# A first stage on two bank pairs, a Gram matrix on four tiles, and convolutions with their taps in turns

## The reference

```
xn  = layernorm(x)
q,k,v = silu(short_conv4(xn @ W.T))            # 4 heads of 64, causal, 4 taps per channel
beta = sigmoid(xn @ Wb.T)
delta = chunked delta rule on l2norm(q), l2norm(k), v*beta, k*beta   # triangular solves, a scan
local = three causal FIR filters over v, of 3, 15 and 63 taps
p   = softmax((xn @ gate_w + gate_b) / exp(log_temp)), clipped mix with eps
o   = p0*short + p1*mid + p2*long + p3*delta + p4*v ;  o = rmsnorm(o) * norm_w
x1  = x + layernorm(o @ Wo.T)
xr, xk = mixes of layernorm(x1) and its row before
out = x1 + layernorm(sigmoid(xr @ Wr) * (relu(xk @ Wk)^2 @ Wv))
```

## Time and profile before

| | us |
|---|---|
| median of 3 runs | 616.0 (615.16 to 617.41) |
| the profiled execution | 611.72 |
| its span | 609.9 |
| TensorE busy (matmul) | 512.3 |
| TensorE busy (weight load) | 407.8 |
| VectorE busy | 465.3 |
| GpSimd busy | 336.4 |
| ScalarE busy | 276.6 |

### The profile page before, as it was taken

The page is one execution under the profiler, slowest core; times in us unless marked ns, Lnnn a source line. Parts: engine busy times, 40 slices in busy tenths (PEclk is TensorE's granted clock), DMA queues, the critical chain, the costliest instruction groups (busy, mean ns, idle before and its releaser), DMA issues.

```text
span 609.9 us, 23551 instructions
## 1 busy us (share of the span) xinstructions
PE 512.3 (84%) x9580; PEld 407.8 (67%) x9580; DVE 465.3 (76%) x1182; ACT 276.6 (45%) x688; POOL 336.4 (55%) x408
## 2 busy tenths in 40 slices
PE   2888848999889789798999979899787899888764
PEld 1666636666667567677777767777666777777553
DVE  3788684655589673788899989899768879889863
ACT  5788882111355443435455444454342444433421
POOL 9966202877702440486626378464278776566622
PEclk9999997999999795899999999999888899999978
DMA  9729444699344425341444624165343244333101
GB/s 286 204 71 258 144 139 121 156 225 227 64 73 75 81 63 100 52 72 37 98 88 92 121 52 80 44 120 105 67 72 69 51 104 76 70 80 80 37 17 35
DMA packets 155707, 61.10 MB, mean 100 GB/s; under 512 B 125009, under 2 KB 147409, under 8 KB 155601
## 3 DMA queue, kind: packets, MB, share of 16 engines
q1 hardware_dynamic: 155600, 59.61, 44.5%
HBM read 40.62 MB, written 18.95 MB: 98 GB/s over the span
## 4 chain that ended last, share of the span: by engine, by line
PE 29%; DVE 23%; issue 17%; POOL 13%; SPq 7%; DMA 6%; ACT 3%; POOLq 0%; DVEq 0%; ACTq 0%
PE bank L1864 6%; PE bank L1639 5%; DVE cva L1126 4%; DVE arena L1236 3%; PE bank L1553 3%; POOL arena L659 3%; PE bank L1901 3%; DVE arena L1350 3%; PE bank L1718 2%; DVE arena L1365 2%; DVE arena L1338 2%; POOL seq L650 2%; POOL seq L561 2%; PE bank L1758 2%; POOL seq L648 2%
## 5 line engine op out<-in xcount | busy, mean ns | idle before, releaser
L659 POOL TENSOR_TENSOR arena<-arena,neg_half 128x2 f32<-128x2 f32 (+1 forms) x64 | 61.2, 956 | 148.4 <-DVE arena L1325 88.1
L1236 DVE SCALAR_TENSOR_TENSOR arena<-bank,small,arena 128x256 f32<-128x256 f32 x192 | 89.9, 481 | 15.5 <-ACT arena L898 10.6
L1210 DVE TENSOR_TENSOR seq<-bank,seq 128x384 f32<-128x384 f32 x64 | 35.2, 556 | 30.3 <-PE bank L1639 19.4
L606 POOL TENSOR_TENSOR arena<-seq,powers 128x16 f32<-128x16 f32 x16 | 48.6, 3040 | 17.0 <-DVE seq L1252 17.0
L1639 PE MATMUL bank<-arena 128*64 128x192 f32 x512 | 50.4, 340 | 3.9 <-DVE seq L1210 1.6
L1126 DVE SCALAR_TENSOR_TENSOR cva<-bank,small,cva 128x256 f32<-128x256 f32 x96 | 40.3, 477 | 15.1 <-ACT cva L775 14.8
L577 POOL TENSOR_TENSOR seq<-seq 128x256 f32<-128x256 f32 x32 | 23.3, 729 | 48.2 <-DVE seq L1210 48.2
L1639 PEld LDWEIGHTS bank<-arena 128*64 128x64 f32 x512 | 35.4, 140 | 13.4 <-issue 6.3
L1350 DVE TENSOR_SCALAR arena<-arena 128x256 f32<-128x256 f32 x64 | 31.7, 536 | 16.0 <-POOL arena L659 16.0
L898 ACT ACTIVATE arena<-bank,small 128x256 f32<-128x256 f32 x64 | 29.7, 467 | 26.2 <-PE bank L1718 26.2
L1718 PE MATMUL bank<-arena,w_k 128*128 128x268 f32 x128 | 34.5, 412 | 4.4 <-issue 3.1
(11 more groups left out here) (170 smaller groups left out, 1364.5 us busy)
## 6 DMA issues: line engine op xcount, KB each, us to landing
arena<-v_scratch SPq DMA_DIRECT2D x64, 128.0 KB, 3.3
arena<-fl SPq DMA_DIRECT2D x32, 192.0 KB, 6.4
arena<-fms SPq DMA_DIRECT2D x32, 192.0 KB, 6.8
arena<-xnT_scratch SPq DMA_DIRECT2D x32, 134.0 KB, 3.1
arena<-x SPq DMA_DIRECT2D x32, 128.0 KB, 2.9
gram_scratch<-arena SPq DMA_DIRECT2D x32, 128.0 KB, 2.4
out<-arena SPq DMA_DIRECT2D x32, 128.0 KB
xnT_scratch<-seq SPq DMA_DIRECT2D x2, 1027.0 KB, 6.7
```

What stands on the lines that cost most here:

```text
L606: pool.tensor_tensor(rk, ssel[:, slot_of(n)], powers[:, :, :], ALU.pow).then_inc(s["norms"], 1)
L659: pool.tensor_tensor(dst, src, half8 if k == U else neg_half[:, 0:k], ALU.pow).then_inc(s[dst_sem], 1)
L1210: nc.vector.tensor_tensor(fprod[:, q % (2 * FPAIRS), :], bank[fir_bank(q)][:, 0:2 * ROW], fgate[:, q // (TILES // 2), :], ALU.mult).then_i ...
L1236: nc.vector.scalar_tensor_tensor(cv[:, t], ps[:, :, j:j + C], conv_w[:, 1 - t // 2, t % 2, j:j + 1], cv[:, t], ALU.mult, ALU.add).then_inc ...
```

## The change

The first stage gets a second pair of banks (7 and 1) and a second `cva` (`cvx`) for every other quarter. The turned rows use bank 0 alone. VectorE normalizes the first four tiles of batch 0. Gate bias and temperature go into ScalarE's copy. The sums of the gates, the waits before the FIR stage and all orders of the stage move.

```diff
+        def a_bank(q, oh):
+            return bank[(2, 3, 7, 1)[2 * (q % 2) + oh]]
+        def a_row(q, oh):
+            return (cvx if q % 2 else cva)[:, oh, :]
...
-                    if b or q:
-                        pe.wait_ge(s["a_conv"], b * 24 + 6 * (q - 1) + 5 + oh)
+                    if 4 * b + q >= 2:
+                        pe.wait_ge(s["a_conv"], b * 24 + 6 * (q - 2) + 5 + oh)
...
+            def a_first(b):
+                if b == 0:
+                    dve.wait_ge(s["a_rs"], 1)
+                    for m in range(4):
+                        nc.vector.tensor_scalar(xna[:, m, :], xa2[0][:, m, :], mv_a[:, m, 0:1], rs_a[:, m:m + 1],
+                                                ALU.subtract, ALU.mult).then_inc(s["a_first"], 1)
...
-                act.activation(gT, bank[6][:, 0:2 * P], ACT.Copy).then_inc(s["a_gT"], 1)
+                act.wait_ge(s["g_step"], G_READY)
+                act.activation(gT, bank[6][:, 0:2 * P], ACT.Identity, bias=gate_bias, scale=inv_temp).then_inc(s["a_gT"], 1)
...
-                for g in range(5):
-                    for pr in range(PAIRS):
-                        last = nc.vector.tensor_scalar(gates[:, g, pr, :], gates[:, g, pr, :], gb[:, pr, g:g + 1],
-                                                       inv_temp[:, pr:pr + 1], ALU.add, ALU.mult)
```

The Gram step becomes one, on four tiles, with its key part in bank 4:

```diff
-            def gram(m, g):
+            def gram(m):
...
+                for x in KQ:
+                    pe.wait_ge(s["silu_" + x], m + 1)
+                pe.wait_ge(s["at"], m)
+                pe.wait_ge(s["g_tok"], m)
+                if m >= LEAD:
+                    pe.wait_ge(s["oT"], m - LEAD + 1)
+                for u in range(U):
+                    for e in range(2):
+                        keys = kq[slot_of(m)][HH[e], u, 0, :]
+                        mm(bank[2][HH[e], C * u:C * u + C], keys, kq[slot_of(m)][HH[e], u, 1, :], start=True, stop=True)
+                        last = mm(bank[4][HH[1 - e], C * u:C * u + C], keys, keys, start=True, stop=True)
+                last.then_inc(s["gram"], 1)
...
             def scan_kq(n):
+                pe.wait_ge(s["g_tok"], min(n + LEAD, N))
```

`at_parts` and `gram_out` become one operation of 512 columns each. `conv(n, kind)` runs the taps of both halves in turns, and `shifted` is one operation:

```diff
+            def conv(n, kind):
                 for j in range(PAD):
+                    for t in (2 * kind, 2 * kind + 1):
...
+                nc.vector.tensor_tensor(dx.rearrange("p h (b t) -> p h b t", b=B), xf[:, :, :, 1:], xf[:, :, :, 0:C],
+                                        ALU.subtract).then_inc(s["dx"], 1)
```

More of the change, by code:

```diff
@@ L470, in lead_step @@
             def lead_step(n):
[L472 to L485, removed]
@@ L535, in _ @@
-            for n in range(-170, 22):
+                if 0 <= n + 6 < 2:
+                    diag_in(n + 6)
+                    products_in(n + 6)
+                if 0 <= n + 18 < 1:
+                    values_in(n + 18)
+                    direct_in(n + 18)
+                if FIRST <= n + 27 < FIRST + 4:
+                    toep_late(n + 27)
+                if 0 <= n + 2 < 2:
+                    solved_in(n + 2)
+                if n - 1 < 0 and solving(n - 1) is not None:
+                    solved_store(solving(n - 1))
@@ new lines, in tail_step @@
+            def tail_step(n):
+                if 10 <= n - 15 < N:
+                    diag_in(n - 15)
+                if 7 <= n - 19 < N:
+                    rows_out(n - 19)
+                if 9 <= n - 15 < N:
+                    values_in(n - 15)
+                    direct_in(n - 15)
+                if n - 18 >= 8 and solving(n - 18) is not None:
+                    solved_store(solving(n - 18))
+                if 9 <= n - 16 < N:
+                    rows_in(n - 16)
+                if 10 <= n - 14 < N:
+                    solved_in(n - 14)
+                    products_in(n - 14)
@@ L536, in _ @@
+            for n in range(-164, 35):
                 lead_step(n)
@@ L1025, in chunk_step @@
-            def chunk_step(n):
+                if 0 <= n + 21 < 8:
+                    gram_out(n + 21)
+                    square(n + 21, 3)
+                    square(n + 21, 2)
+                if 0 <= n + 12 < 1:
+                    low_out(n + 12)
+                if 0 <= n + 22 < 8:
+                    tap(n + 22, 0)
+                    silu(n + 22, 1)
+                    tap(n + 22, 2)
+                    tap(n + 22, 3)
+                    silu(n + 22, 0)
+                    silu(n + 22, 2)
+                    silu(n + 22, 3)
@@ L1512, in tail_step @@
                     o_normed(n)
+                if 7 <= n - 1 < N:
+                    mix(n - 1, 0, xr)
                 if 7 <= n - 2 < N:
```

911 lines of the change are left out of this document (427 added, 484 removed).

## The result

The changed kernel takes 619.5 us (median of 20 runs, 614.9 to 624.4) where the kernel before takes 615.5 (20 runs): ratio 1.0083 [1.0060, 1.0106], about 5 us slower. The ratios leave out each kernel's slow runs, those over 1.5% above its fastest, so the medians (4.0 us apart) and the ratio differ a little. The forecast was 607, so it failed in size and in sign.

What follows compares the result with a forecast made beforehand. TensorE and VectorE bind the chunk loop; no engine is full in first stage or lead. First stage -9.4, lead +6.5, start-up -1, loop -5 sum to -8.9 us: 602.8 profiled, 607 against the median, range 598 to 616.

Steps and rivals of the forecast that it cites:

- First stage: Everything before the FIR stage: start, batches, gate bias and fgate wait together 9.4 us earlier (5 to 13).
- Start: First stage: VectorE normalizing the first four tiles itself brings the first convolution 2.4 us earlier (1 to 3.5).
- End, the gate bias: First stage's end: bias and scale operations moved into ScalarE's gate copy save 2.8 us on the path (2 to 3).
- The fgate wait: Before the FIR stage: gates' copy and first product no longer wait for a store of v, 0.9 us (0.5 to 1.2).
- Batches: First stage: projection leaves the wait cycle, a batch takes 16.7 to 17.2 us, not 17.62; 3.3 us over four (1 to 6).
- rival B: ScalarE holds the first stage, its window copies preceding the tap; loop gains only 2; 612.5 or up to 615; chance 0.15.
- Lead: Before the scan: new orders lengthen a chunk from 7.13 to 9.3 us; scan start moves 6.5 us later (0 to +12).
- rival C: Lead: TensorE's gaps halve its clock for six of eight chunks, 12 us a chunk, 16 us more, 623; chance 0.13.
- Loop: Chunk loop: TensorE and VectorE lose about 0.9 of 24.0 us, 0.6 per chunk remains, 5 us earlier over eight chunks.
- Turns and the drain: VectorE's convolutions: taps in turns take 2.56 us for six against 2.95 in series; by the drain rule they gain nothing.
- Start-up: Start-up of the scan, after the lead: gains 1 us.
- tail: After the chunk loop: the recurrence keeps its members, so 0 us change (-3 to +3).

Runs made afterwards that it cites:

- e1: The changed kernel's new first stage alone, with lead, loop and tail of the kernel before: 608.3 us, ratio 0.9874 to the kernel before.
- e3: The changed kernel with another order of convolutions, masks, silus, taps and projections in the lead alone: 613.1 us, ratio 0.9981 to the kernel before.
- e7: e5 and e6 together: 603.2 us, ratio 0.9799 to the kernel before.
- e2: First stage of the kernel before, with the changed kernel's lead, loop and tail: 628.6 us, ratio 1.0203 to the kernel before.
- e5: The changed kernel with x normalized earlier in VectorE's loop order, ahead of diagonal sums, solved-block turn and key convolution: 622.5 us, ratio 1.0090 to the kernel before.
- e12: e10 with SyncE's diagonal load ahead and x normalized earlier except in the two chunks with a solve: 596.9 us, ratio 0.9718 to the kernel before.
- e4: The changed kernel with each tensor's three taps in series again in lead and loop: 628.5 us, ratio 1.0206 to the kernel before.
- e8: The kernel before with only the loop's convolution pairs taking taps in turns and one difference of shifted rows: 620.0 us, ratio 1.0057.
- e10: e6 with the last two silus of v ahead of the gates' exponential on ScalarE: 598.9 us, ratio 0.9711 to the kernel before.
- e6: e3 with SyncE's lead loads and stores reordered and the scaling of the blocks moved: 602.5 us, ratio 0.9759 to the kernel before.

## Why the prediction was wrong

*First stage, 9.4 forecast, 5.0 in the profile.* Start: 16.34 to 14.07, 2.3 of 2.4, right. End, the gate bias: from the third convolution of the last batch to the fourth 6.5 us instead of 9.3, 2.8 of 2.8, right. The fgate wait: 0.9 forecast, 0.16 found. The copy that waited for the store was not the last input: in the changed kernel it waits for TensorE's turn of the gates behind the first FIR tile. Batches: 3.3 forecast and -0.2 found (1.4 in e1's trace, so this term varies from one execution to the next; over the traces of e1 and e3 to e7, which share this stage, the first FIR product comes 4.9 to 7.1 us earlier than before). The step that failed is "ten and 5.3 us of work plus the waits": it gave the freed waits to the batch, and they were taken by input rows and by taps behind ScalarE's copies (it works without a gap worth 0.1 us from 65.99 to the late tap at 69.06), as rival B had it in part. By the runs e1 is nonetheless 1.26% [0.68, 1.84] faster, 7.8 us, within which my 9.4 lies.

*Lead, +6.5 forecast, +10.4.* The period was right (9.3, measured 9.4), and so was the walk to the load of the solved block, 8.7 us later relative to the lead (72.9 against 64.2). The failed sentence is "TensorE was busy with Gram and sums until 233 before, so the start of the scan moves by 6.5 us, not 8.7". It took the end of TensorE's work in the lead as fixed, though the period that I had just lengthened holds for all eight chunks. In the changed kernel the load is issued and the scan's first matmul comes only 8 us later, right behind the eighth Gram step in TensorE's order:

```profile
230.14 1.93 SPq L454 DMA_DIRECT2D arena<-solved_scratch  x4
238.44 1.05 PE L1790 MATMUL bank<-arena,seq 16*32 16x16 f32 x64
```

That missed chain alone would not have moved the number much. Seven periods of 9.37 from the first mask operation would be 65.6 us; they are 70.9. Of the 5.3 us more, some 4.3 are falls of the clock, rival C's mechanism in three of seven periods (1.4, 2.0 and about 1.0 us; I had asked for six of eight); the other 1.0 is the last period's own, which takes 10.4 us in e2 at full speed too. Without the falls, by this estimate, the eighth Gram step would have ended 76.9 us into the lead and the scan started about 6 us later than before, near the forecast. The solved block, issued to 232.07 and 2.0 us (median) in landing, was there at about 76.8, so the two chains are level. What is over the 6.5 is therefore the clock, which the sum had at nothing. e2's trace repeats it: 81.1 us from the first projection to the scan, as here, with 4.2 us lost in two periods.

*Loop, -5 forecast, +5.3.* Here the sign fell, and this is the step that failed most: "So 0.6 per chunk remains". The size of the work was right: TensorE 1.2 us less per period, undisturbed period 23.2. Against that, over seven periods of e2 and of before: TensorE's work 8.3 us less (seven times the 1.19 of the quiet period), waits for the other engines 7.8 more, issue 1.2 more, clock 3.4 more. That is +4.1 of the 5.0 measured in e2; it is a sum read from traces. By experiment, taking waits away made single periods shorter (e5, e12), but the best loop, e12's 168.0, only equals that of the kernel before. I had written one wait of 0.6 per period. The mean period of e2 is 24.7, above the 24.0 that the prediction itself named as the sign of being wrong. TensorE's wait for VectorE is 0.5 to 0.9 in a quiet period, and 2.5 to 4.4 in the fourth, sixth and seventh, where a load or the solve makes VectorE late. These periods have their own chains (a DMA behind SyncE's wait for the solve, GpSimd's square roots behind the solve), and I took one chunk in the middle of the loop for all eight. The clock was priced in the lead alone.

*Turns and the drain.* The Trainium skill's rule, "VectorE: DVE Perf Modes", The DRAIN you can't avoid, would have turns gain nothing. Six taps take 2.44 us in turns here and 2.95 in series, so VectorE does gain; by e4 and e8 the loop doesn't, for another reason.

*Start-up* +0.5 for -1, and *tail* -2.2 for 0 (-3 to +3): small both. The tail's new orders are the one place that beat the forecast.

No rival gave the result: B and C each held in a part, and neither reached the loop's loss (B had its gain shrink to 2). What stays open is why TensorE's clock falls in two to four of the loop's seven periods in all kernels with the new orders and in none of the first six periods of the kernel before, which has issue pauses as long (1.4 us) and one wait of 1.7. Also open is how much of the loop's loss belongs to the Gram step on four tiles and how much to the new orders around it: neither was run without the other.

## What to carry to other kernels

When a shared order is lengthened, walk it to its last member as well as to the one you are interested in: here the chain over the eighth chunk came out level with the one over the fourth, and falls of the clock, which the sum left out, made it the last. A loop whose periods differ (a solve every fourth chunk, loads behind it) must be priced in its worst periods, since a wait that is harmless in the quiet ones is what a thinner TensorE runs into. And before a new instruction order is judged, look at the queue that feeds it: e3's order was worth 1% with the old load queue and 3.2% with the loads that nobody waits for yet moved behind the urgent ones.

## What the runs showed of the hardware

In e2's loop TensorE's granted clock fell from 2.4 to 1.2 GHz three times, each time within 1 us after a stand of 1.09, 1.35 or 2.48 us, and each fall cost 1.7 us of work. The length of the last stand does not decide it: in the same trace a stand of 1.83 us was followed by full speed, and so was one of 1.7 us in the kernel before.

```profile
302.79 0.25 PE L1786 MATMUL bank<-arena 32*32 32x32 f32 x4 [1.09 <-issue]
...
350.81 0.37 PE L1786 MATMUL bank<-arena 32*32 32x32 f32 x10 [1.35 <-issue]
...
381.98 1.15 PE L1814 MATMUL bank<-arena 64*64 64x64 f32 x32 [1.83 <-DVE arena L1294]
```

```profile
351.20:354.00 2.80, 2.80 (x81) 2.80 (x84) 1.67 (x7) 0.81 (x2) 0.69 (x1) 0.50 0.31 59
...
382.00:386.00 4.00, 2.94 (x160) 2.64 (x160) 4.00 (x10) 0.87 (x2) 3.61 (x8) 1.00 0.97 220
```

And ScalarE's order of activation functions costs: the exponential ahead of the last two silus put two table loads of 1.28 us in front of them, and silu first took both away from that path and delayed the exponential by 0.5 us at most (e10 against e6).
